# Cross-attention and a token-shift FFN on one core: W_q turned by VectorE in 32x32 blocks, keys and W_q K^T in strips of 32, key sums as a 155th column

## The reference

```
xn  = layernorm(x)
q   = xn @ Wq ; k = ctx @ Wk ; v = ctx @ Wv          # per head, 128 wide
sim = q @ k.T / sqrt(128)
sim = (sim - mean_j(sim)) * 1.5 + mean_j(sim)
x   = x + softmax(sim) @ v @ Wout + bout
xn  = layernorm(x) ; xr, xk = mixes of xn with the token before (mu_r, mu_k)
x   = x + sigmoid(xr @ W_r.T) * (relu(xk @ W_k.T)**2 @ W_v.T)
```

## Time and profile before

| | |
|---|---|
| median of 3 runs | 745.97 us (744.39 to 746.34) |
| the profiled execution | 745.34 us, its span 743.5 us |
| TensorE busy | 738.0 us (99%), 3964 matmul records |
| VectorE, ScalarE busy | 514.3 us (69%), 427.9 us (58%) |
| granted TensorE clock | 1.00 over the span |
| opening, up to tile 1's turn | 32 us |

### The profile page before, as it was taken

One profiled execution on the slowest core, in us unless ns is written; L12 is line 12 of the kernel. 1 busy time (PEld: TensorE's weight loads), 2 busy tenths in 40 slices (PEclk: granted clock), 3 DMA queues, 4 the chain that ended last, 5 costly groups with the idle time before them and its releaser, 6 DMA issues.

```text
span 743.5 us, 13579 instructions
## 1 busy us (share of the span) xinstructions
PE 738.0 (99%) x3964; PEld 645.4 (87%) x3964; DVE 514.3 (69%) x1081; ACT 427.9 (58%) x1204; POOL 123.3 (17%) x279
## 2 busy tenths in 40 slices
PE   9999999999999999999999999999999999999998
PEld 8958888888988888898888889888888988888887
DVE  3678897867667766666776766677666667766662
ACT  3569866575646556564655656465565646565332
POOL 1112011202121120212112021211202121120211
PEclk9999999999999999999999999999999999999999
DMA  9973644445444353545435354533535454343301
GB/s 338 253 207 103 207 136 133 147 130 176 139 135 153 119 159 95 176 139 163 129 113 158 96 176 141 165 121 120 164 87 175 144 166 127 112 154 93 111 29 43
DMA packets 85655, 106.52 MB, mean 143 GB/s; under 512 B 9951, under 2 KB 62073, under 8 KB 85627
## 3 DMA queue, kind: packets, MB, share of 16 engines
q1 hardware_dynamic: 85588, 106.15, 46.6%
q10 hardware_dynamic: 39, 0.04, 0.0%
HBM read 58.70 MB, written 47.45 MB: 143 GB/s over the span
## 4 chain that ended last, share of the span: by engine, by line
PE 94%; ACT 2%; DVE 2%; issue 1%; POOL 0%; POOLq 0%; DVEq 0%; ACTq 0%
PE ffn L496 12%; PE ffn L498 12%; PE ffn L497 12%; PE scores L497 9%; PE scores L498 9%; PE scores L496 9%; PE attended L498 8%; PE attended L497 8%; PE attended L496 8%; PE scores L652 1%; PE attended L546 1%; PE attended L545 1%; PE scores L683 1%; PE scores L714 1%; PE ffn L714 1%
## 5 line engine op out<-in xcount | busy, mean ns | idle before, releaser
L497 PE MATMUL scores<-A_lo,xT_hi 128*128 128x462 f32 x372 | 130.4, 351 | 0.0
L496 PE MATMUL scores<-A_hi,xT_hi 128*128 128x462 f32 x372 | 130.0, 350 | 0.4 <-ACT probs L787 0.4
L498 PE MATMUL scores<-A_hi,xT_lo 128*128 128x462 f32 x372 | 130.0, 349 | 0.0
L787 ACT ACTIVATE probs<-scores,neg_max 128x154 f32<-128x154 f32 x248 | 93.4, 388 | 47.7 <-DVE neg_max L1044 47.6
L496 PE MATMUL attended<-B_hi,pT_hi 128*128 128x512 f32 x288 | 112.2, 389 | 0.4 <-DVE pT_lo L984 0.4
L498 PE MATMUL attended<-B_hi,pT_lo 128*128 128x512 f32 x288 | 112.5, 391 | 0.0
L497 PE MATMUL attended<-B_lo,pT_hi 128*128 128x512 f32 x288 | 112.4, 390 | 0.0
L1044 DVE TENSOR_REDUCE neg_max<-scores 128x3 f32<-128x462 f32 (+1 forms) x93 | 53.5, 582 | 85.1 <-PE scores L498 85.1
L1339 POOL TENSOR_SCALAR var<-stats 128x1 f32<-128x1 f32 x64 | 12.4, 194 | 460.8 <-DVE stats L990 459.7
L496 PEld LDWEIGHTS scores<-A_hi,xT_hi 128*128 128x128 f32 x372 | 70.2, 189 | 7.7 <-issue 1.4
L497 PEld LDWEIGHTS scores<-A_lo,xT_hi 128*128 128x128 f32 x372 | 70.1, 188 | 5.6
(11 more groups left out here) (176 smaller groups left out, 1585.3 us busy)
## 6 DMA issues: line engine op xcount, KB each, us to landing
prob_rows<-probs SPq DMA_DIRECT2D x32, 704.0 KB, 4.0
probs_handed<-prob_rows SPq DMA_DIRECT2D x128, 176.0 KB, 3.4
x_rows<-normed SPq DMA_DIRECT2D x61, 256.0 KB, 3.2
handed<-x_rows SPq DMA_DIRECT2D x244, 64.0 KB, 1.9
x_in<-in_x SPq DMA_DIRECT2D x32, 256.0 KB, 2.9
out<-x SPq DMA_DIRECT2D x31, 256.0 KB, 3.6
wq<-in_L_xattn_Wq SPq DMA_DIRECT2D x2, 1024.0 KB, 10.1
wout<-in_L_xattn_Wout SPq DMA_DIRECT2D x1, 2048.0 KB, 19.9
```

Source lines behind the costliest of these rows:

```text
L496: te.matmul(psum, left[0], right[0], start=first, stop=False)
L497: te.matmul(psum, left[0], right[1], start=False, stop=False)
L498: return te.matmul(psum, left[1], right[0], start=False, stop=last)
L787: last = nc.scalar.activation(probs[:, q, cols], score_banks(t)[b][:, (h - h0) * J:(h - h0 + 1) * J], ACT.Exp, bias=neg_max[:, h:h + 1], a ...
```

## The change

**Loading.** W_q comes in eight DMAs instead of two. Partitions 32q to 32q+31 receive columns 256q to 256q+255 (heads 2q and 2q+1); the first four DMAs bring rows 0 to 255, the others rows 256 to 511; a piece is 1 KB.

**Turning.** TensorE's transposes of W_q and the copies that follow them are gone. VectorE turns blocks of 32x32 from SBUF to SBUF, `queries_turn(c, e)`: 128 x 512 elements a call, eight calls, for chunk c and head 2q+e of every quarter. `wqT[32q.., slot, :]` then holds 32 columns of a head: slot 4e + b, columns 32b to 32b+31 of head 2q+e. Their place in VectorE's order is part of the change: the first before the first key shift, the second after it, four after the shifts, the last two between the low parts of chunks 1 and 2; the statistics of tile 1 move behind the low part of chunk 2.

**Keys.** K^T is laid out in the same way: each of 24 products of 128 columns becomes four of 32 columns, written to four strips of partitions of one bank.

**Products.** For each chunk and slot, four products contract over 32 rows each and write to four banks (`A_BANKS` is now T + O and S + XB); four slots b are accumulated, so a bank ends with two heads of 154 columns. High and low parts are four of 308 columns per chunk. `turn_x(0)` writes to O and so waits for the low parts of chunk 2; the values go to the T banks.

**Sums.** Six matmuls of one column add the sum over ctx's tokens as a 155th column of ctx^T, so K^T's sum arrives as column 155 of each slot; the three reductions are gone.

```diff
@@ sync
-            wq_rows = Wq.rearrange("(c p) n -> p c n", p=P)
+            wq_rows = Wq.rearrange("(b i) (q n) -> q i b n", i=Q, q=4)
...
-                cols = slice(4 * i * P, 4 * (i + 1) * P)
-                sp.dma_start(wq[:, :, cols], wq_rows[:, :, cols]).then_inc(wq_loaded[i], 16)
+                half = slice(2 * DC * i, 2 * DC * (i + 1))
+                for q in range(4):
+                    sp.dma_start(wq[q * Q:(q + 1) * Q, half, :], wq_rows[q][:, half, :]).then_inc(wq_loaded[i], 16)
@@ tensor
+            for c in range(CC):
+                total = XB[:, c * KJ + J:(c + 1) * KJ]
+                te.matmul(total, ctx0[:, c * P:(c + 1) * P], normed[:, 0:1], start=True, stop=False)
+                last = te.matmul(total, ctx1[:, c * P:(c + 1) * P], normed[0:J - P, 0:1], start=False, stop=True)
...
-                    for h in range(h0, h1):
-                        last = te.matmul(S[b][:, (h - h0) * J:(h - h0 + 1) * J], wk[:, c, h * P:(h + 1) * P],
-                                         ctxT[:, c, :], start=(c == 0 and h == h0), stop=(c == CC - 1 and h == h1 - 1))
+                    for slot in range(s0, s1):
+                        for q in range(4):
+                            at = (2 * q + slot // 4) * P + slot % 4 * Q
+                            last = te.matmul(S[b][q * Q:(q + 1) * Q, (slot - s0) * KJ:(slot - s0 + 1) * KJ],
+                                             wk[:, c, at:at + Q], ctxT[:, c, :],
+                                             start=(c == 0 and slot == s0), stop=(c == CC - 1 and slot == s1 - 1))
...
-            for h in range(HEADS):
-                te.wait_ge(wq_loaded[h // 4], 16)
...
-                for c in range(DC):
-                    last = te.transpose(WQ_BANKS[h % len(WQ_BANKS)][:, c * P:(c + 1) * P],
-                                        wq[:, c, h * P:(h + 1) * P], identity[:])
-                last.then_inc(wq_turned, 1)
...
             for c in range(DC):
                 if c >= 2:
-                    te.wait_ge(A_ready, 3 * (c - 1))
+                    te.wait_ge(A_ready, 4 * (c - 1))
+                for e in range(2):
+                    te.wait_ge(wq_turned, 2 * c + e + 1)
+                    for b in range(4):
+                        slot = 4 * e + b
+                        if c == 0:
+                            te.wait_ge(kT_ready, 3 if e or b == 3 else slot // HPB + 1)
+                        for q in range(4):
+                            rows = slice(q * Q, (q + 1) * Q)
+                            last = te.matmul(A_BANKS[c % 2][q][:, e * J:(e + 1) * J],
+                                             wqT[rows, slot, c * P:(c + 1) * P], kT[rows, slot, :],
+                                             start=b == 0, stop=b == 3)
+                last.then_inc(A_done, 1)
+            te.wait_ge(A_ready, 4 * (DC - 1))
             turn_x(0)
@@ scalar
-            for h in range(1, HEADS, 2):
-                act_e.wait_ge(wq_turned, h + 1)
-                copy(wqT[:, h, :], WQ_BANKS[h % len(WQ_BANKS)][:]).then_inc(wqT_odd_ready, 1)
             for c in range(DC):
...
+                act_e.wait_ge(A_done, c + 1)
+                for q in range(4):
+                    copy(A_hi[:, c, q * QK:(q + 1) * QK], A_BANKS[c % 2][q][:, 0:QK]).then_inc(A_hi_ready, 1)
@@ vector
+            def queries_turn(c, e):
+                dve.wait_ge(wq_loaded[c // 2], 64)
+                to = wqT[:, 4 * e:4 * e + 4, c * P:(c + 1) * P].rearrange("p b (r i) -> p r b i", i=Q)
+                rows = wq[:, 4 * c:4 * c + 4, e * P:(e + 1) * P].rearrange("p r (b i) -> p r b i", i=Q)
+                v.transpose(to, rows).then_inc(wq_turned, 1)
...
+            queries_turn(0, 0)
+            keys_shift(0)
+            queries_turn(0, 1)
+            keys_shift(1)
+            keys_shift(2)
+            for c in (1, 2):
+                for e in range(2):
+                    queries_turn(c, e)
             x_statistics(0, 0, 1)
...
+            for c in range(2):
+                product_lo(c)
+            for e in range(2):
+                queries_turn(3, e)
+            product_lo(2)
+            x_statistics(1, 1, 1)
+            product_lo(3)
             x_lo(0)
```

More of the change, by code:

```diff
@@ L39, in xattn_ffn @@
     HJ = HEADS * J
+    KJ = J + 1
     QK = 2 * J
@@ L188, in xattn_ffn @@
         assert at_mix + size_of([P, HEADS, D]) <= at_act
-        ctxT = sb("ctxT", [P, CC, J], at=at_probs_handed)
+        ctxT = sb("ctxT", [P, CC, KJ], at=at_probs_handed)
         x1T = (sb("x1T_hi", [P, DC, P], F32R, at=at_gate), sb("x1T_lo", [P, DC, P], F32R, at=at_gate + size_of([P, D])))
@@ L318, in score_banks @@
             return T if isinstance(t, int) and t == 1 else S
-        WQ_BANKS = T + [XB]
-        A_BANKS = [S, T]
-        V_BANKS = [XB, T[0], T[1]]
+        A_BANKS = [T + [O], S + [XB]]
+        V_BANKS = T
         B_BANKS = [S[0], S[1], S[2], XB]
@@ L726, in _ @@
                         last = te.matmul(V_BANKS[b][:, (h - h0) * J:(h - h0 + 1) * J], wv[:, c, h * P:(h + 1) * P],
-                                         ctxT[:, c, :], start=(c == 0), stop=(c == CC - 1))
+                                         ctxT[:, c, 0:J], start=(c == 0), stop=(c == CC - 1))
                 last.then_inc(values_done, 1)
             turn_x(1)
-            te.wait_ge(A_ready, 3 * DC)
+            te.wait_ge(A_ready, 4 * DC)
             scores(0)
@@ L897, in _ @@
             act_e.wait_ge(ctxT_turned, 1)
-            copy(ctxT[:], XB[:, 0:CC * J].rearrange("p (c j) -> p c j", j=J)).then_inc(ctxT_ready, 1)
+            copy(ctxT[:], XB[:, 0:CC * KJ].rearrange("p (c j) -> p c j", j=KJ)).then_inc(ctxT_ready, 1)
             for b, (h0, h1) in enumerate(HEAD_BANKS):
@@ L901, in _ @@
                 for h in range(h0, h1):
[L902 removed]
+                    last = nc.scalar.activation(kT[:, h, :], S[b][:, (h - h0) * KJ:(h - h0) * KJ + J], ACT.Identity,
                                                 bias=key_shift[:, h:h + 1], scale=STRETCH * SCALE)
                 last.then_inc(kT_ready, 1)
[L905 to L907 removed]
             for c in range(DC):
[L909 to L911 removed]
+                act_e.wait_ge(A_done, c + 1)
+                for q in range(4):
+                    copy(A_hi[:, c, q * QK:(q + 1) * QK], A_BANKS[c % 2][q][:, 0:QK]).then_inc(A_hi_ready, 1)
                 if c == 0:
@@ L1221, in _, with keys_shift @@
             v.memset(normed[:, 0:P], 1.0).then_inc(busy_ready, 1)
-            for b, (h0, h1) in enumerate(HEAD_BANKS):
+            def keys_shift(b):
+                h0, h1 = HEAD_BANKS[b]
                 dve.wait_ge(keys_done, b + 1)
[L1224 to L1227, removed]
+                totals = S[b][:, 0:(h1 - h0) * KJ].rearrange("p (h j) -> p h j", j=KJ)[:, :, J]
+                v.tensor_scalar(key_shift[:, h0:h1], totals, (1.0 - STRETCH) * SCALE / J, None, ALU.mult
@@ new lines, in product_lo @@
+            def product_lo(c):
+                for q in range(4):
+                    dve.wait_ge(A_hi_ready, 4 * c + q + 1)
+                    low_part(A_lo[:, c, q * QK:(q + 1) * QK], A_BANKS[c % 2][q][:, 0:QK],
+                             A_hi[:, c, q * QK:(q + 1) * QK]).then_inc(A_ready, 1)
+            queries_turn(0, 0)
[6 more added lines that the diff above has]
+                    queries_turn(c, e)
```

33 lines of the change are left out of this document (6 added, 27 removed).

## The result

The kernel after took 752.9 us (median of six runs, 750.95 to 756.88), the kernel before 745.29 on the same chip: ratio 1.0106 [1.0087, 1.0125]. It is 1.1% slower; the forecast was no change, 744.2 to 749.2. The profiled execution took 750.95 us, its span 749.2, 5.7 more than before's 743.5.

What follows compares the result with a forecast made beforehand. TensorE, 99% busy, bounds the opening; of 4.1 us gained, 1.2 go to totals, the rest to VectorE's order, moving tile 0's turn +0.4 us (D = 1.65) or -0.75 (D = 0). Forecast 745.8 us, range 744.2 to 749.2, 76%.

Steps and rivals of the forecast that it cites:

- D: Extra transfer time of W_q in 1 KB pieces: 1.65 us, likely band 0 to 1.65, upper bound 5.0.
- the rival that ended on the slower side: W_q lands late, delaying chunk 2's turns and the probabilities: +3.75 us at D = 5.0, 749.7; 12%.
- four run together: Key products in four 32-column strips run four abreast: 24 x 0.262 us, up to 7.3 us in all.
- The clock comes up later: Rival: one-column products do little, so keys run at half pace; three us of that cost 1.5, 747.3; 5%.
- Key totals: Six one-column matmuls on TensorE's path before the keys: 1.2 us, bounds nothing to 3.5 us.
- Strips of rows four abreast: W_q K^T products in 32-row strips run four together: 2.1 us per chunk, as before the change.
- the rival of serial weight loads: Row strips' weight loads go one after another: +5.1 us on TensorE, partly swallowed, 748 to 748.8; 10%.
- VectorE's order: W_q turns, statistics and low parts on VectorE make TensorE wait at slot 3 and ahead of chunks 2 and 3.
- A shift passes one for one: A shift of the opening reaches the kernel's end undiminished, if the probabilities are in SBUF by then.
- Values: TensorE's value products after tile 0's turn: 6.3 us of work, covering tile 1's late statistics by 1 us.
- Probabilities: Reload of the probabilities through SP's queue, wanted by VectorE at 57.45: 1.6 us of cover; covered at D = 1.65.
- The gain: TensorE loses 32 W_q transposes and their wait, 4.1 us gross; tile 0's turn -0.75 us at D = 0.

Runs made afterwards that it cites:

- The experiments with either thing alone: Kernel before, W_q in 2 KB pieces into 32 partitions: 751.63 us, 1.0077; changed kernel, W_q in 1 KB pieces into 128 partitions: 753.08 us, 1.0103.
- repairing the load: Changed kernel with W_q loaded in two DMAs of 2 KB pieces over 128 partitions, as before the change: 753.1 us, 1.0116.
- the loads held: Changed kernel with two wide W_q loads, wide keys and reductions, plus loads from Wout on held until A is complete: 758.89 us, late by design.

## Why the prediction was wrong

**The step that failed is the transfer of W_q.** "A straight line between gives 55 ns for 1 KB, 295 GB/s", D = 1.65, with 5.0 as the upper bound. Measured: 20.18 against 14.3, D = 5.9, outside even the bound. The two windows of the earlier trace rows differ in two things, piece and number of partitions; I put all of it down to the piece. Their second window had the right rate, 201 GB/s, and the rival that ended on the slower side named the 32 partitions, but gave them 12% and priced them from the same bound, 749.7. The experiments with either thing alone settle it. Why it was worse still than that bound: the rate was 211 to 235 GB/s up to 18 us, which alone makes 2.1 MB take 9 to 10 us against 5.45; in the last 2.6 us the queues moved 362 GB/s, most of it already what was queued behind. That the last quarter shared the engines with those loads is my reading of these two rows, not shown by a run. The prediction also took its 201 GB/s to contradict the rule of 512 bytes that it cites. It doesn't: that window has 32 partitions as well, and no run here has such pieces in 128.

**A second cause had no term at all: TensorE's stops.** The sum counted the strips by their time in the array and said "four run together". They do. But 24 products became 96 and 32 became 128 (two records each), and their instructions have to be fetched through the same DMA engines that the loads fill. With W_q on time TensorE stands still for 4.0 us in two stops. This, with the half clock behind the second and the totals, is why repairing the load did not help (1.0116), and why each of the causes, measured alone, looks like the whole loss: they lie in parallel, and the later one hides the earlier.

**The clock.** "The clock comes up later" had 5% and 1.5 us. It did, at 0.57 from 7 to 11 us (2.4 GHz only part of the time, else 1.2), and the key strips took 8.21 us instead of 6.5. Its reason, the one-column products, is not borne out: in kernels without them the keys took 8.14 us (wide) and 8.21 and 8.31 (strips), against 7.25 in before, and why they differ stays open. In after that lies under the wait for W_q; with the loads on time the totals make 0.43% between two of the kernels, mostly by starting the keys 3.1 us later. Not foreseen was that a stop can bring half clock again: chunk 0 at 0.25 us a pass until 21.0, the values at 7.99 us. Not every stop does: behind the one of 2.48 us the granted clock stayed at 1.00.

**Key totals**: 1.2 us forecast, 1.86 measured (4.52 to 6.38; six pairs at 0.31), 3.1 at half pace; inside the bounds.

**Strips of rows four abreast**: right, 0.13 us a pass, so the rival of serial weight loads falls. The Trainium skill (TensorE: Matmul & The Clock Gate, Part 3) says that a weight load overlaps products in flight only where its row group differs. This trace agrees: the four loads of a pass run together (0.19 us each, at 21.22) beside the products of the pass before.

**VectorE's order**: right. From the arrival of W_q's second half to tile 0's turn the sum had 9.7 us (15.95 to 25.65); measured 10.7 (20.18 to 30.88), with a stop of 0.69 in it. The normalisation came 3.75 after that arrival in the sum, 3.63 in the trace. **A shift passes one for one**: right, 5.7 at `packed_rows` and in the span. **Values**: 6.33 for 6.3. **Probabilities**: the last quarter was issued by 59.2 and landed within 4.0, against a turn at 63.1; not binding in after, binding as soon as TensorE was 2.2 us earlier.

**The gain.** Of the 4.1 us of transposes, the sum left 0.75 for a load on time. With totals and key strips out of the way as well, the kernel was still slower, 1.0025. With the stops gone too, tile 1's turn came at 32.85, 0.8 us later than in before, and the 24 wide key products took 8.10 us there for 7.25 in before. So no run shows a gain, and none shows that a load on time and without stops would bring none.

**Open.** The six runs of after spread over 5.9 us, those of before over 2. Kernels with the same totals show the keys start at 7.1 to 7.3 or at 8.9 to 9.1, by the pace of the totals (0.31 or 0.52 us a pair), which would account for some 2 us of it, but only the fastest was profiled, so that stays a guess. A kernel with wide keys, W_q in DMAs to 128 partitions and W_q where VectorE's turn needs it was not tried.

## What to carry to other kernels

Count a tiled product by its instructions as well as by its passes: four times as many instructions are four times as many fetches, and beside a saturated load queue a fetch can stop the engine, in these kernels for up to 2.5 us, sometimes with half clock behind it. Give a large load all 128 partitions, and when two windows of a trace differ in two things, bound by the worse one before drawing a line through one of them. When undoing a suspect moves nothing, look for a second cause of the same size before acquitting it.

## What the runs showed of the hardware

A DMA into 32 partitions moved 229 GB/s (1 KB pieces) and 243 (2 KB), or 231 and 227 from 8 to 18 us; into 128 partitions 359 and 385. Two queues that wrote 32 partitions each, one below and one above partition 64, moved 334 together, and one of them alone 201. TensorE's stops go with packets of 16 KB of instructions, moved by DMA: beside full load queues the packet started 2.0 us later than with the loads held, TensorE went on 1.2 to 1.7 us after it had moved, and the stops of over 0.5 us lasted 0.69 to 2.48 us; in the one execution with the loads held there was none. Products of one column ran at 0.31 us a pair in two kernels and at 0.52 in four others with the same code, although the granted clock reads 1.00 in all six from 3 to 7 us. Four products of 32 rows took 0.13 us a pass of 154 columns, as the four strips of 32 columns do.
